# A conditioned transformer block on one core: new orders of the first and last batch, one division an iteration, and a part of x's stack on ScalarE

## What is computed

```python
mod = swish(c) @ w_mod + b_mod                      # six rows of 144 for each batch
sh_msa, sc_msa, g_msa, sh_mlp, sc_mlp, g_mlp = split(mod, 6)
xn = _ln(x) * (1 + sc_msa) + sh_msa
q, k, v = heads(xn @ w_qkv + b_qkv)
q, k = _ln(q, g_q), _ln(k, g_k)                     # over the 9 channels of a head
o = softmax(q @ k.T * 9 ** -0.5) @ v
x = x + g_msa * (o @ w_proj + b_proj)
xn2 = _ln(x) * (1 + sc_mlp) + sh_mlp
h = gelu(xn2 @ w1 + b1)
x = x + g_mlp * (h @ w2 + b2)
```

## Time and profile before

| | |
|---|---|
| median of 3 runs | 188.19 (187.58 to 188.20) |
| the profiled execution | 189.93 |
| its span from first to last instruction | 188.1 |
| TensorE busy | 161.7, 86% |
| VectorE busy | 138.3, 74% |
| ScalarE busy | 101.1, 54% |
| GpSimd busy | 72.4, 39% |
| mean granted clock of TensorE | 0.963 |

### The profile page before, as it was taken

The page is one execution under the profiler, slowest core; times in us unless marked ns, Lnnn a source line. Parts: engine busy times, 40 slices in busy tenths (PEclk is TensorE's granted clock), DMA queues, the critical chain, the costliest instruction groups (busy, mean ns, idle before and its releaser), DMA issues.

```text
span 188.1 us, 3898 instructions
## 1 busy us (share of the span) xinstructions
PE 161.7 (86%) x1483; PEld 90.8 (48%) x1483; DVE 138.3 (74%) x351; ACT 101.1 (54%) x130; POOL 72.4 (39%) x92
## 2 busy tenths in 40 slices
PE   7999867807978989989889889898699699999983
PEld 2524324303524435535335444444254596969672
DVE  4479599465776899999969999999977656944111
ACT  3040040872695798897776688986675213060410
POOL 8205921359129548174292240504354144400000
PEclk9999999985996999999969999999999999999999
DMA  3638489500000000000000000000000000110101
GB/s 67 210 88 269 99 287 369 162 0 0 3 2 0 3 0 0 3 0 5 0 0 3 0 3 0 0 5 0 0 5 0 0 3 0 63 66 0 63 0 63
DMA packets 4595, 8.67 MB, mean 46 GB/s; under 512 B 881, under 2 KB 3131, under 8 KB 4466
## 3 DMA queue, kind: packets, MB, share of 16 engines
q1 hardware_dynamic: 4288, 8.41, 14.2%
q10 hardware_dynamic: 288, 0.01, 0.1%
HBM read 7.21 MB, written 1.21 MB: 45 GB/s over the span
## 4 chain that ended last, share of the span: by engine, by line
PE 44%; DVE 38%; issue 8%; POOL 5%; ACT 4%; POOLq 0%
PE ps_o L1265 8%; PE ps_x L1045 8%; PE ps_o L1161 6%; PE ps_s L1248 5%; PE ps_x L1084 5%; DVE kst L773 4%; PE ps_s L1146 4%; DVE o_nrm L861 3%; DVE ssum L746 3%; PE ps_o L1070 2%; DVE xT L741 2%; DVE kn L758 2%; DVE kst L770 2%; DVE bst L880 2%; PE ps_x L1077 2%
## 5 line engine op out<-in xcount | busy, mean ns | idle before, releaser
L583 ACT ACTIVATE pTs<-ps_s,escale 128x1024 f32<-128x1024 f32 x64 | 68.0, 1111 | 25.0 <-PE ps_s L1146 24.1
L1161 PE MATMUL ps_o<-pTs,v 128*32 128x256 f32 x512 | 39.1, 410 | 3.2 <-DVE o_blk L853 2.9
L1146 PE MATMUL ps_s<-qT,kT 32*128 32x256 f16 x256 | 25.0, 279 | 4.4 <-ACT pTs L583 3.1
L631 ACT ACTIVATE late<-ps_s 120x512 f32<-120x512 f32 (+1 forms) x20 | 11.9, 596 | 26.7 <-PE ps_s L1248 26.7
L1045 PE MATMUL ps_x<-idle_z 128*128 128x512 f16 x75 | 19.9, 425 | 2.7 <-ACT raw L555 1.5
L1161 PEld LDWEIGHTS ps_o<-pTs,v 128*32 128x32 f32 x512 | 13.1, 113 | 18.3 <-issue 10.2
L1265 PE MATMUL ps_o<-w_sb,late 120*128 120x144 f32 (+1 forms) x160 | 20.5, 287 | 0.9 <-ACT late L631 0.7
L1265 PEld LDWEIGHTS ps_o<-w_sb,late 120*128 120x128 f32 (+1 forms) x160 | 19.9, 190 | 1.6 <-ACT late L631 1.2
L1248 PE MATMUL ps_s<-late,w1s 110*120 110x512 f16 (+1 forms) x80 | 18.5, 380 | 0.3 <-issue 0.3
L371 POOL TENSOR_SCALAR z<-xall,mv,rstd 128x144 f32<-128x144 f32 x14 | 16.2, 1162 | 5.8 <-DVE rstd L1322 5.8
L1146 PEld LDWEIGHTS ps_s<-qT,kT 32*128 32x128 f16 x256 | 7.4, 93 | 22.2 <-issue 10.4
(11 more groups left out here) (121 smaller groups left out, 251.4 us busy)
## 6 DMA issues: line engine op xcount, KB each, us to landing
mbc<-mod_rows SPq DMA_DIRECT2D x6, 432.0 KB, 7.8
late<-in_w SPq DMA_DIRECT2D x1, 990.0 KB
xall<-in_x SPq DMA_DIRECT2D x1, 864.0 KB, 5.0
out<-late SPq DMA_DIRECT2D x3, 288.0 KB, 2.2
z2s<-in_w_qkv SPq DMA_DIRECT2D x1, 742.5 KB
mbc<-mod_rows SPq DMA_DIRECT2D x2, 288.0 KB, 6.7
pTs<-in_w_mod SPq DMA_DIRECT2D x1, 486.0 KB
w_sb<-in_w SPq DMA_DIRECT2D x1, 337.5 KB
```

What stands on the lines that cost most here:

```text
L583: nc.scalar.activation(pT[u % NP].rearrange("p g n -> p (g n)"), ps_s[:, 2 * (u % 2):2 * (u % 2) + 2, :].rearrange("p a n -> p (a n)"), AC ...
L631: nc.scalar.activation(hT[k % 2][0:FW[f], f, :], ps_s[0:FW[f], (NF * k + f) % 4, :], ACT.Gelu_apprx_tanh, scale=UNSCALE).then_inc(gelued, 1)
L1146: mm = nc.tensor.matmul(ps_s[:, 2 * (u % 2) + a, half * N:(half + 1) * N], kT[par][rows, j, i * P:(i + 1) * P], qT[par][rows, j, :], start ...
L1161: mm = nc.tensor.matmul(ps_o[SLOT * g:SLOT * (g + 1), 1, (j % 2) * N:(j % 2 + 1) * N], v[par][:, i, h, :], pT[u % NP][:, g, :], start=(i = ...
```

## The change

- **VectorE's buffers.** o_blk, rden, o_nrm and o_ch become one tensor each, so that both pairs can be named in one instruction.
- **One division an iteration.** `normalise(n)` now takes the first pair of batch n and the second of batch n-1 together: one reciprocal, two multiplies, one transpose of 512 columns to two slices of o_ch. `project(n)` waits for the `normalise` of n+1. After the last batch a half is done alone.
- **ScalarE makes the high part.** For batches 3 to 7 the cast at line 732 is done by ScalarE (`high_part`), behind the last exponential of iteration n for batch n+3. It waits for xm, for TensorE's transposes of the batch before and for VectorE's copy of xT. VectorE does only the low part.
- **First batch.** VectorE's stack of batch 2 moves from the front of iteration 0 to the place behind `k_out`. TensorE does scores 5 and values 2 ahead of k's transposes.
- **Opening.** 18 filler matmuls where there were 38.
- **Last two batches.** VectorE: `first_half_z` comes ahead of `normalise` in iteration 6; in the end part the second pair of batch 6 is normalised with the first of batch 7, `standardise2(1)` comes behind `zT_half(0, 1)`, and the last half is normalised behind `zT_half(1, 0)`. TensorE: values 4 and scores 6 come ahead of the first transposes of z, and `project(6)` behind scores 7.

```diff
+            def high_part(b):
+                act.wait_ge(prep.mx.sem, prep.mx.after(b, "xm"))
+                act.wait_ge(prep.xpe.sem, prep.xpe.after(b - 1, "xT"))
+                act.wait_ge(prep.x.sem, prep.x.after(b - 1, "xT"))
+                nc.scalar.activation(xst[:, :, 0:3 * CW].rearrange("p t (s w) -> p t s w", w=CW)[:, :, 0:3:2, :],
+                                     xm[:].rearrange("p i (c w) -> p (i c) w", w=CW).unsqueeze(2)
+                                     .broadcast_to([P, I * NC, 2, CW]), ACT.Copy).then_inc(prep.x.sem, 1)
...
                 exponentials(n, 7)
+                if n + 3 < B:
+                    high_part(n + 3)
...
+                if S is pre or b < 3:
+                    nc.vector.tensor_copy(slots[:, :, 0:3:2, :], xc.unsqueeze(2).broadcast_to([P, I * NC, 2, CW])
+                                          ).then_inc(S.x.sem, 1)
...
+            def normalise(n, pairs=slice(0, 2)):
+                last = min(2 * n + 1, 2 * B)
+                dve.wait_ge(o_out, last)
+                c = pairs.stop - pairs.start
+                nc.vector.reciprocal(rden[:, pairs], o_blk[:, pairs, :, :, HD]).then_inc(post_dve.sem, 1)
+                dve.wait_ge(post_dve.sem, post_dve.after(n, "rd"))
+                for pair in range(pairs.start, pairs.stop):
+                    mul = nc.vector.tensor_tensor(o_nrm[:, pair, :, 0:2 * HD].rearrange("p b (j d) -> p j b d", j=2),
+                                                  o_blk[:, pair, :, :, 0:HD],
+                                                  rden[:, pair].unsqueeze(3).broadcast_to([P, 2, QB, HD]), ALU.mult)
+                    mul.then_inc(halves_done, 1)
+                dve.wait_ge(halves_done, last)
+                if n >= 3:
+                    dve.wait_ge(post_pe.sem, post_pe.after(n - 3, "proj"))
+                if pairs.start == 0 and n >= 2:
                     dve.wait_ge(post_pe.sem, post_pe.after(n - 2, "proj"))
+                if c == 2:
+                    to = o_ch[:, 0:4:3] if n % 2 == 0 else o_ch[:, 1:3]
+                else:
+                    k = 2 + (n - 1) % 2 if pairs.start else n % 2
+                    to = o_ch[:, k:k + 1]
+                nc.vector.transpose(to, o_nrm[:, pairs].rearrange("p k b s -> p k (b s)")).then_inc(post_dve.sem, 2)
...
-                if ahead and first:
-                    stack(n + 2, prep)
                 if not first:
                     blocks(n - 1, 1)
...
+                if first:
+                    stack(n + 2, prep)
                 blocks(n, 0)
...
-                if not first:
-                    normalise(n - 1, 1)
-                normalise(n, 0)
+                if n == B - 2:
+                    first_half_z()
+                normalise(n, slice(0, 1) if first else slice(0, 2))
                 if n >= 2:
                     statistics(n - 2)
                 if ahead and n + 3 < B:
                     stack(n + 3, prep)
-                if n == B - 2:
-                    first_half_z()
...
-            normalise(B - 2, 1)
             stack2(0)
             blocks(B - 1, 0)
             zT_half(0, 0)
-            normalise(B - 1, 0)
+            normalise(B - 1)
+            zT_half(0, 1)
             standardise2(1)
-            zT_half(0, 1)
...
             blocks(B - 1, 1)
-            normalise(B - 1, 1)
             zT_half(1, 0)
+            normalise(B, slice(1, 2))
             zT_half(1, 1)
...
-            keep_busy(38)
+            keep_busy(18)
             pe.wait_ge(set_dve.sem, set_dve.after(0, "wq"))
...
             def project(n):
-                pe.wait_ge(post_dve.sem, post_dve.after(n, "oc1"))
+                pe.wait_ge(post_dve.sem, post_dve.after(n + 1, "oc"))
...
                 scores(n, 4, par)
+                if first:
+                    scores(n, 5, par)
+                    values(n, 2, par)
                 if makes:
                     qkv_used(n + 1, prep)
                     transpose_k(n + 1, prep)
-                scores(n, 5, par)
-                values(n, 2, par)
+                if not first:
+                    scores(n, 5, par)
+                    values(n, 2, par)
                 values(n, 3, par)
...
             scores(n, 5, par)
+            values(n, 4, par)
+            scores(n, 6, par)
             pe.wait_ge(res_dve.sem, res_dve.after(n - 2, "x1"))
             transpose_z_half(0, 0)
-            values(n, 4, par)
-            scores(n, 6, par)
-            project(n - 1)
             values(n, 5, par)
             scores(n, 7, par)
+            project(n - 1)
             transpose_z_half(0, 1)
```

39 lines of the change are left out of this document (12 added, 27 removed).

## The result

| | before | after |
|---|---|---|
| median of the runs | 188.19 (187.58 to 190.07, with the profiled one) | 192.81 (191.03 to 192.91) |
| ratio, 95% interval | | 1.021 [1.013, 1.029] |
| the profiled execution | 189.93 | 191.03 |
| its span | 188.1 | 189.2 |
| busy TensorE, VectorE | 161.7, 138.3 | 160.6, 134.6 |

The account below looks back on a forecast made before the run. It took a closed loop of TensorE work and ScalarE and VectorE latency, period 11.87, as the bound. 188.1 - 1.8 - 1.5 - 3.0 + 1.3 + 1.2 + 1.3 = 185.6, own range 184.2 to 187.1, wider range 182.6 to 188.8.

Parts of the forecast that it names:

- The plain iteration: Loop over batches: VectorE does 0.9 less work, but the period stays 11.87, so 0 is saved per plain iteration.
- Rival (a): Loop: VectorE is the bound after all, so four iterations shrink by 2.6 in all, giving 183.0; chance 0.25 together with another case.
- w1's pieces: Two iterations where VectorE does a piece of w1 before the sums: 0.9 less VectorE work each, -1.8.
- the clock's part: Behind w1's first piece: a shorter wait keeps the granted clock from falling, -1.5, with 0 as the other end.
- The first batch: Batch 0's new orders: Newton starts earlier and TensorE's idle stretch is filled, -3.0; half lost if the clock recovers no sooner.
- The opening: Twenty fewer fillers save nothing, and the clock falls before the first QKV matmuls: +1.3, ends -0.6 and +3.2.
- rival (c): After the opening the clock stays down, slowing further fillers and k's transposes and shrinking later gains: 190.6; chance 0.13.
- The last two batches: Batches 6 and 7: +1.2 for a multiply blocked by GpSimd and +1.3 for z of the second quarter made later.
- a blocked multiply: Batch 6: one VectorE multiply of o meets GpSimd's steps, ahead of the blocks batch 7's values need: +1.2, ends 0 and +2.4.
- the late z: Batch 7: z of the second quarter ends at 141.0, not 138.3, delaying the second hidden matmuls: +1.3, between 0.3 and 2.
- The signs: Stated checks: loop period, sums after w1, k's transposes near 41.5, clock at first QKV, batch 6 multiply, wait before project(6).

Follow-up runs that it names:

- b_same: The kernel before, unchanged, run once more for a second trace; 187.39, span 185.6.
- b_first: The kernel before with only the new orders of the first batch; median 188.13, ratio to before 0.984.
- b_fill: The kernel before with 16 filler matmuls ahead of k's transposes of batch 1; 189.10 against 189.86 for before in the same group.
- b_open18: The kernel before with 18 opening fillers in place of 38, nothing else changed; median 194.23.
- a_open38: The kernel after with 38 opening fillers again, nothing else undone; median 190.98.
- a_both: The kernel after with 38 opening fillers and the first quarter's z behind batch 6's normalisation again; median 188.21, ratio to before 0.998.
- a_z_after: The kernel after with only the first quarter's z back behind normalisation and statistics in iteration 6; median 193.05, ratio to before 1.024.
- c_open18: c_oldtail with 18 opening fillers in place of 38; median 187.64.
- c_oldtail: a_open38 with batches 6 and 7 in the old order, with the old single halves; median 184.92, ratio to before 0.970.
- a_three: a_both with z of the second quarter again ahead of the copy of z's second transposed half; median 185.46, ratio to before 0.986.
- c_dve: c_oldtail with VectorE instead of ScalarE making the high part for every batch; median 186.96.
- c_oldtail_fill: c_oldtail with 8 filler matmuls on TensorE in iteration 0, between values 1 and scores 4; median 183.00, ratio to before 0.966.

## Why the prediction was wrong

**The plain iteration: right.** It was said to stay 11.87 with VectorE idle 0.8 before the sums; it is 11.87 and 0.82. Rival (a), VectorE as the bound, is refuted by the same rows. The copy on ScalarE takes 0.68 against 0.65 estimated, and the squares still start 0.04 behind the QKV matmuls.

**w1's pieces: the saving right, the clock's part only for some executions.** Said: sums 0.27 behind the squares, -1.8; measured 0.40, 14.55 + 13.04 to twice 12.22, -3.15, with the fall's 1.5 in it. In b_same, b_first and b_fill, which have no fall there, these iterations take 13.03 to 13.05, so against such an execution the gain is 2 x 13.04 - 2 x 12.22 = 1.6, and the term of -1.5 is nothing. Two traces of the old loop have a fall behind w1's first piece (the profiled execution of before and b_open18), three have none, and none of the nine traces with the new loop has one.

**The first batch: right in its kind, smaller than said.** Said -3.0. The profiled pair gives 16.16 - 13.34 = 2.8, and the other new traces with a fall of 6.8 there 13.55 to 13.88, so 2.3 to 2.6. Where the fall lasts 10.2 the new order takes 16.04 (a_open38) and 16.18 (a_both) against 16.67 in b_same, a gain of 0.5 to 0.6. That is less than the lower end of the prediction, half of the gain (1.4).

**The opening: right that the cut saves nothing, mis-sized.** Said +1.3; from the end of wq to the squares it is 6.24 to 6.34 in the four kernels with 18 fillers against 4.42 to 4.44, so +1.8 to +1.9. (The table at the top has +1.23, as wq itself was ready 0.58 sooner in that execution, 19.79 and not 20.37.) More can come behind it, 1.1 (a_z_after, c_open18) to 2.7 (b_open18) in the next iteration. The prediction had that as rival (c) at 0.13. Three of the four traces with 18 fillers show it; that of after doesn't.

**The last two batches: here it failed.** The prediction had +1.2 for a blocked multiply and +1.3 for the late z, together +2.5. From the squares of batch 7 to the second hidden matmuls it is +6.27: +4.61 to the first hidden matmuls and +1.66 behind them. TensorE's time from the squares of batch 7 to the first hidden matmuls, taken apart into busy and idle:

| kernel | stretch | busy | idle | time at 1.2 GHz in it |
|---|---|---|---|---|
| before, b_same | 23.2 | 20.07 | 3.2 | 0 |
| c_open18 (new loop, old order here) | 22.92 | 20.08 | 2.84 | 0 |
| c_oldtail (the same order) | 25.82 | 22.98 | 2.84 | 6.8 |
| a_three (joint halves, later project(6)) | 24.89 | 19.97 | 4.92 | 0 |
| a_both (and the late z) | 26.57 | 22.57 | 4.00 | 6.8 |
| a_open38 (and project(5) waits) | 26.91 | 21.54 | 5.37 | 3.4 |
| after | 27.85 | 22.79 | 5.06 | 6.8 |

- **The waits.** a_three idles 1.75 more than before: 1.52 before project(6) (said: 1.4), and 1.68 for `blocks` where before waits 1.12 for zst. The prediction saw the first and let the hidden matmuls begin "near 139.9" all the same. This is the first part of **the failing step**: a wait that stands on TensorE's path to the hidden matmuls was put at nothing, and it costs 1.7 to 2.0 (24.89 against 23.24 and 22.92).
- **The clock.** The sum has no term for a fall of the clock in batch 7; before had none there. After's fall of 6.8 makes TensorE 22.79 busy and not 20.07, **+2.7**. This is the second part of the failing step, and the larger. The order alone doesn't bring it: with the old order here c_oldtail and c_dve have the same fall and pay 2.9.
- **project(5).** The change made `project(n)` wait for `normalise(n + 1)` and in the same edit put z's 1.65 and a collision of 1.66 - 0.53 = 1.13 in front of it. The collision's size was about as forecast; its consumer was missing. But its wait of 1.98 mostly takes the place of others: the one for `blocks` behind it shrinks from 1.68 to 0.61, and all idle together is 0.1 (after) to 0.5 (a_open38) above a_three's. So the collision, said to cost 1.2, costs TensorE 0.1 to 0.5 of waiting. Whether this wait brings the fall on stays open: the fall began in the wait, but a_z_after, without the wait, had a fall as long 8.6 later.

From the first to the second hidden matmuls it is 10.53 against 8.87, +1.66 (said: 150.4 - 148.82 = 1.6, of which the sum took 1.3). a_three, which makes z earlier, has 8.31, so the late z costs 2.2 to 2.3 against it. Here the date, 150.4, was even met (150.33), but that is luck: the loop's gain had moved batch 7's beginning from 116.71 to 111.95, and all of it was lost on the way.

Between traces without any fall in batch 7, c_open18 takes 31.79 from the squares to the second hidden matmuls and a_three 33.20, so the joint halves and the later project(6) cost 1.4; with the late z's 2.2 the new orders cost 3.6 at the full clock. After takes 38.38, 3.0 beyond that, and 2.8 of it is busy time at 1.2 GHz ahead of the first hidden matmuls (22.79 against a_three's 19.97).

The signs that the prediction named nearly all came true (the period, the clock at the first QKV, a wait of 1.52 before project(6), two multiplies in 1.66 in batch 6; k's transposes at 43.18 - 1.23 = 41.95 and not 41.5). None of them looked at the clock or the waits of batch 7 as a whole, so they couldn't show that the time was wrong.

**The sum against the wrong execution.** The prediction took the sum, which is a span, for the median, since span and median were both 188.1. Time is span plus 1.8, so the median of before corresponds to a span of 186.4 (188.19 - 1.8), and the profiled execution was one of its long ones. The profile of after was one of its short ones (191.03; the others 192.7 to 192.9). Between these two profiles lies +1.1, between the medians +4.6. An account from one profile to another can be right in each term and still miss by 3.5. No trace shows where the other four executions of after spend their 1.7 to 1.9 more: two of them have as much time at 1.2 GHz as the profiled one (24), two have 28.

**What makes up the median, in steps.** after 192.81; filler back 190.98; z of iteration 6 back 188.21; z of the last batch back 185.46; the halves and project(6) back 184.92. These are differences of medians, partly from different groups (before had 188.52, 188.31 and 189.86 in those of a_both, a_three and c_oldtail), each with its clock in it, and their order was chosen; a_z_after shows that the second step alone gives nothing. Open is what decides where the clock falls in batch 7: after, a_open38, a_z_after, a_both, c_oldtail, c_dve, c_oldtail_fill and b_fill had a fall there, and before, b_same, b_first, b_open18, a_three and c_open18 had none.

## What to carry to other kernels

When an edit lets a consumer wait for a later step of another engine (project for the next normalise), write down for every batch, the last ones too, what now stands before that step; a step that has an iteration to spare in the loop may have none where the order changes. Then see what the wait takes the place of: here 1.98 of it cost 0.1 to 0.5. Comparing TensorE's busy and idle time in one stretch of two kernels tells the order's cost (idle) from the clock's (busy). Taking filler out of an idle stretch of TensorE can cost more than it seems: 1.9 at once and up to 2.7 behind it here. And before a forecast is summed from one profile, see how span and granted clock of several executions lie: here one program (a_both) had spans from 185.5 to 191.1, and traces without a fall in the stretch in question told the parts apart where medians did not.

## What the runs showed of the hardware

- **Two outcomes of one program.** a_both ran seven times at 187.3 to 188.6 and four times at 192.8 to 193.0, with 10 to 18 and 24 microseconds at 1.2 GHz. The Trainium skill (TensorE: Matmul & The Clock Gate, What's actually happening) says that the number of cold matmuls at a kernel's start varies from run to run with the phase of the gate, and puts the penalty of this ramp at under 1% of a typical kernel's span. That the time at the lower level varies from run to run agrees; but these falls lie in the middle of the kernel, and the two outcomes are 2.6% apart.
- **What TensorE did before a fall of the clock.** In a_z_after, from 129 to 133 ahead of the fall at 133.4, it was busy 2.00 of 4.00, with no gap longer than 1.68. In the kernel before, ahead of the fall at 58.2, it was busy 1.29 from 56 to 58. In after the fall came 1.6 into an idle stretch of 1.98. a_three waited the same 1.68 for `blocks` in batch 7, and its clock stayed at 1.00.
- **GpSimd and VectorE.** Beside a GpSimd multiply (line 492) two multiplies of o took 1.66 and not 0.53, and beside GpSimd's addition of xm a small Newton step 0.84 and not 0.22. By the Trainium skill (SBUF — State Buffer, Who interferes with whom) two inputs in SBUF are what meets GpSimd's reads; the multiplies have o_blk and rden as inputs and the Newton step ssum and qnt, and the trace agrees.
- **ScalarE's copy** of 576 elements from SBUF to SBUF with a cast takes 0.68, VectorE's 0.44.
